# Spectral mixing kernel on one Trainium2 core: reordering at the three seams between its stages

## The reference

```
xf = rfft2(x, axes=(1, 2), norm='ortho')            # (4, 128, 65, 768), complex
o1 = relu(xf @ w1 + b1)                             # complex product, relu on each part
o2 = softshrink(o1 @ w2 + b2, 0.01)                 # complex product, per part
out = irfft2(o2, s=(128, 128), axes=(1, 2), norm='ortho') + x
```

## Time and profile before

| | us |
|---|---|
| median of 3 runs | 5172.28 (5172.27 to 5175.37) |
| profiled execution | 5172.48 |
| its span | 5170.2 |
| TensorE busy | 5031.5 |
| VectorE busy | 3993.2 |
| ScalarE busy | 2508.0 |
| GpSimd busy | 627.2 |

### The profile page before, as it was taken

How to read it: one execution, slowest core, us unless ns; L and a number is a source line. 1 busy time by engine, 2 the same in 40 slices (tenths; PEclk the granted TensorE clock), 3 DMA queues, 4 the chain that set the end, 5 groups by cost and what they waited for, 6 DMA issues and landing times.

```text
span 5170.2 us, 111909 instructions
## 1 busy us (share of the span) xinstructions
PE 5031.5 (97%) x43072; PEld 4143.5 (80%) x43072; DVE 3993.2 (77%) x5987; ACT 2508.0 (49%) x3649; POOL 627.2 (12%) x420
## 2 busy tenths in 40 slices
PE   7999999999999999999999999999999999999999
PEld 6887878888787887878878887888878778887887
DVE  6778777787777877778777787777787777877777
ACT  4554544545455454554445544445445455454543
POOL 0111011110111101111011110011110111101111
PEclk9999999999999999999999999999999999999999
DMA  3331233312333113332133321333312333123311
GB/s 107 99 99 36 73 100 99 104 44 61 100 99 104 50 54 99 99 104 61 44 100 99 104 74 43 87 99 104 89 41 74 99 104 99 44 61 99 103 50 50
DMA packets 1067748, 421.11 MB, mean 81 GB/s; under 512 B 1064864, under 2 KB 1064992, under 8 KB 1067168
## 3 DMA queue, kind: packets, MB, share of 16 engines
q1 hardware_dynamic: 1062432, 411.63, 30.1%
q10 hardware_dynamic: 4736, 1.60, 0.1%
HBM read 210.26 MB, written 201.33 MB: 80 GB/s over the span
## 4 chain that ended last, share of the span: by engine, by line
issue 88%; POOL 12%; POOLq 0%; DVE 0%
POOL x L926 12%; POOLq L925 0%; POOLq L929 0%; DVE x L855 0%; POOLq L926 0%; POOLq L938 0%
## 5 line engine op out<-in xcount | busy, mean ns | idle before, releaser
L926 POOL TENSOR_TENSOR x<-shrink_or_v,x 128x480 f32<-128x480 f32 (+1 forms) x416 | 627.0, 1507 | 4534.8 <-DVE shrink_or_v L848 4494.8
L543 PE MATMUL ps<-wts,hbig 128*128 128x192 f32 x4160 | 734.9, 327 | 4.3
L820 DVE TENSOR_TENSOR shrink_or_v<-ps,wts 128x768 f32<-128x768 f32 (+1 forms) x544 | 501.0, 921 | 281.5 <-PE ps L552 254.7
L773 DVE COPY ydg<-ps 128x512 f32<-128x512 f32 (+5 forms) x768 | 504.5, 657 | 250.8 <-PE ps L447 151.8
L447 PE MATMUL ps<-tab,ring 128*128 128x128 f32 x6144 | 694.6, 276 | 0.0
L447 PEld LDWEIGHTS ps<-tab,ring 128*128 128x128 f32 x6144 | 688.5, 192 | 5.4 <-DVE ring L894 5.4
L543 PEld LDWEIGHTS ps<-wts,hbig 128*128 128x128 f32 x4160 | 671.4, 190 | 16.5 <-ACT hbig L688 13.7
L434 PE MATMUL ps<-tab,ring 128*64 128x128 f32 x6144 | 681.6, 274 | 2.4 <-ACT ring L628 2.4
L435 PE MATMUL ps<-tab,ring 128*63 128x128 f32 x6144 | 681.6, 274 | 0.0
L434 PEld LDWEIGHTS ps<-tab,ring 128*64 128x64 f32 x6144 | 672.2, 137 | 7.3 <-ACT ring L628 4.2
L435 PEld LDWEIGHTS ps<-tab,ring 128*63 128x63 f32 x6144 | 672.1, 136 | 0.0
(11 more groups left out here) (71 smaller groups left out, 7507.0 us busy)
## 6 DMA issues: line engine op xcount, KB each, us to landing
out<-x SPq DMA_DIRECT2D x352, 480.0 KB, 4.6
x<-in_x SPq DMA_DIRECT2D x192, 768.0 KB, 7.9
x<-in_x SPq DMA_DIRECT2D x32, 816.0 KB, 8.1
x<-in_x SPq DMA_DIRECT2D x32, 720.0 KB, 6.4
out<-x SPq DMA_DIRECT2D x32, 432.0 KB, 4.2
wts<-in_mix SPq DMA_DIRECT2D x16, 513.0 KB, 3.6
out<-x SPq DMA_DIRECT2D x32, 240.0 KB, 4.4
out<-x SPq DMA_DIRECT2D x32, 192.0 KB, 4.3
```

What stands on the lines that cost most here:

```text
L543: mm = pe.matmul(o, hbig[:, k * H:(k + 1) * H], mix_part("w2_big"), start=first, stop=False, skip_group_check=True)
L773: dve.tensor_copy(*line_moves(stage, g)).then_inc(line_dve, 1)
L820: dve.tensor_tensor(parts(v), d, b2, ALU.add).then_inc(bias_done, 1)
L926: pool.tensor_tensor(xs[p][:, a:b, :], ucopy[g % 4][:, 0:b - a, :], mirror(xs[p], a, b), ALU.add).then_inc(plus_ready, 1)
```

## The change

- In pass it = 1 the second half of unit 1 is transformed ahead of mix1_whole of unit 0, not behind it; and mix1_whole waits for zsmall_ready only ahead of L501.
- The merge stands ahead of mix2_whole of the last unit, in the place of two keep_warm products; behind mix2_rows stand five keep_warm products and no longer the merge and three.
- The first row group runs over channels 0 to 87 (line groups 0 to 21) once these are moved, and over the other 8 channels when all are. Its signals come with the second part.
- The banks of the row groups, of row 0 and of the forward line groups are rotated by two, so that the first row group takes banks 2 and 3, those of inverse line groups 18 and 19.

```
+FIRST_LINES = 22
-        ROW0_BANK = 2
+        ROW0_BANK = 4
         def line_bank(stage, g):
             return (g + ROW0_BANK + 1) % 8 if stage == 0 else g % 8
+        def row_bank(g):
+            return 2 * ((g + 1) % 4)
...
-                def lines_moved(q, stage):
+                def lines_moved(q, stage, g=NG - 1):
                     for who in ("act", "dve"):
-                        pe.wait_ge(line_sems[who], moved_count(q, stage, NG - 1, who))
+                        pe.wait_ge(line_sems[who], moved_count(q, stage, g, who))
...
                 def mix1_whole(q, u):
                     pe.wait_ge(zbig_ready, NP * q + last_part(u))
-                    pe.wait_ge(zsmall_ready, NU * q + u + 1)
                     pe.wait_ge(zhi_ready, NU * q + u + 1)
...
                     pe.wait_ge(zlo_ready, NU * q + u + 1)
+                    pe.wait_ge(zsmall_ready, NU * q + u + 1)
...
                 def rows(q, g):
-                    bank = 2 * (g % 4)
+                    bank = row_bank(g)
...
+                def first_rows(q):
+                    a, b = odd_rows(0)
+                    c = LINE_GROUPS[FIRST_LINES][0]
+                    v, u = (ps[:, row_bank(0) + i, 0:n * CB].rearrange("p (h c) -> p h c", c=CB)
+                            for i, n in ((1, b - a), (0, HG)))
+                    yv, yu = ydg[:, HC + a - 1:HC + b - 1, :], ydg[:, 0:HG, :]
+                    lines_moved(q, 1, FIRST_LINES - 1)
+                    pe.matmul(v[:, :, 0:c], mat("inv_w_odd"), yv[:, :, 0:c], start=True, stop=True)
+                    pe.matmul(u[:, :, 0:c], mat("inv_w_even"), yu[:, :, 0:c], start=True, stop=True)
+                    lines_moved(q, 1)
+                    pe.matmul(v[:, :, c:CB], mat("inv_w_odd"), yv[:, :, c:CB], start=True, stop=True).then_inc(v_done, 1)
+                    pe.matmul(u[:, :, c:CB], mat("inv_w_even"), yu[:, :, c:CB], start=True, stop=True).then_inc(u_done, 1)
...
                                 pe.wait_ge(w1lo_ready, t + 1)
+                            if it == 1:
+                                fwd_big(q, it, 1)
                             if it >= 1:
                                 mix1_whole(q, it - 1)
-                            if (it, 1) in PARTS:
+                            if it != 1 and (it, 1) in PARTS:
                                 fwd_big(q, it, 1)
...
                         mix1_rows(q, NU - 1)
-                        keep_warm(q, 2)
+                        merge(q)
                         mix2_whole(q, NU - 1)
                         mix2_rows(q, NU - 1)
-                        merge(q)
-                        keep_warm(q, 3)
+                        keep_warm(q, 5)
                         inverse_lines(q)
-                        lines_moved(q, 1)
-                        for g in range(NF):
+                        first_rows(q)
+                        for g in range(1, NF):
                             rows(q, g)
...
-                    u, v = (ps[:, 2 * (g % 4) + i, 0:HG * CB].rearrange("p (h c) -> p h c", c=CB) for i in (0, 1))
+                    u, v = (ps[:, row_bank(g) + i, 0:HG * CB].rearrange("p (h c) -> p h c", c=CB) for i in (0, 1))
```

## The result

| | us |
|---|---|
| before, median of 4 runs | 5173.64 (5172.27 to 5175.37) |
| after, median of 4 runs | 5122.28 (5120.02 to 5126.10) |
| ratio, after to before | 0.9902, 95% interval 0.9889 to 0.9916 |
| profiled execution of after | 5123.14, its span 5120.9 |

The change makes the kernel faster by 1.0%. Profiled execution against profiled execution it is 49.3 us, where the sum forecast 72.4. The time is 22 us above the forecast of 5100 and 0.3 us outside the range.

The account below looks back on a forecast made before the run. TensorE, busy 97% of the span at full clock, was taken as the bound; 53.4 + 3 + 1.6 + 14.4 = 72.4 us off the profiled 5172.48 gave 5100, range 5085 to 5122.

Parts of the forecast that it names:

- What bounds the kernel, and the sign: TensorE, busy 97% at full clock, gains only from its waits or unneeded work; faster by over 0.2% at 0.95.
- Rivals 1, 3 and 4: Stall moved to L501, 5122, 8%; merge ahead of last mix2 stalls, 5183, 2%; moves bound otherwise, 5170, 3%.
- rival 2: Split of the first row group gives nothing, short passes eating the wait's gain: 14 us less, 5114; chance 12%.
- rival 1: TensorE stands at L501 because the two remainders come later than now: 22 us back, about 5122; chance 8%.
- First seam: H transform and first mixing: reordering and the later wait gain 1.67 us a step, bounds 1.50 and 1.80, 53.4 in all.
- Even steps: VectorE's earlier folds shorten TensorE's L468 waits for the small remainder: 3 us of 5.3 in all, bounds 0 and 5.3.
- Second seam: Edges, merge ahead of the last mix2_whole: between -0.1 and +0.15 us a step, taken 0.05, 1.6 in all.
- Third seam: First row group split to hide the last move's wait: 0.45 us a step, bounds 0.08 and 0.72, 14.4 in all.
- The cover of keep_warm: Ahead of the inverse lines, five keep_warm end before the tail pack, costing nothing; without that cover, 1.12 us.

Follow-up runs that it names:

- h_only: The kernel before with only unit 1's second half moved ahead of the first mixing and the small remainder's wait placed later: 5132.84 us, ratio 0.9920.
- rot: The kernel after with VectorE's loop turned, so the jump back lies behind the even step's three folds of unit 1: 5103.69 us, ratio 0.9867.
- spread: The kernel after with the third fold moved from unit 1 to unit 2 and later folds one unit on: 5102.71 us, ratio 0.9863.
- m_only: The kernel before with only the merge moved ahead of the last mix2_whole and five keep_warm behind: 5175.71 us, ratio 1.0003.
- nomerge: spread with the merge back in its old place, behind mix2: 5101.15 us, ratio 0.9861.
- r_only: The kernel before with only the split of the first row group and the rotated banks: 5160.65 us, ratio 0.9974.
- nosplit: spread with the first row group undivided, the banks still rotated: 5115.66 us, ratio 0.9888.
- nowarm: spread without the five keep_warm products ahead of the inverse lines: 5124.03 us, ratio 0.9907.
- light: The kernel after with each of the eight transfers of a later load cut to one row of H: 5102.88 us, ratio 0.9866.

## Why the prediction was right and where it failed
- **What bounds the kernel, and the sign:** right. TensorE's waits were the thing to look at, and both large ones went, with no new one at L501 (now L507), L494 (L499) or in front of the last mixing. Rivals 1, 3 and 4 did not come about, nor did rival 2: the rows gain. That rival 1 had put the time at 5122, where it came out, is a coincidence: its stall at L501 isn't there, and the time was lost in another place.
- **First seam:** forecast 1.67 a step, bounds 1.50 and 1.80. Measured 1.75 on the timeline and 1.82 over a step's mixing in h_only, at the upper bound. The timeline shows where the difference lies: the 16 passes of unit 1 now stand together and take 1.81 us (1487.30 to 1489.11) where the sum had 0.99 + 0.98, and the mixing behind them takes 2.27 where it had 2.19. That fits a change of weight width which now falls behind the mixing and no longer into the second half.
- **Even steps: this is the step that failed.** It read "VectorE's start on the folds comes earlier by more than TensorE's need does, so I take 3 us of the 5.3". VectorE was indeed free 1.19 us earlier against TensorE. But I took the 1.85 us of waiting for nothing in the earlier trace rows as a constant. It is the loop's jump, whose length depends on the loads, less what still runs beside it: 3.73 in the same step after, and the folds began 0.7 us later, not 1.2 earlier. I had weighed late loads only as data for the folds, by their issue and landing, and that was right: rot's first fold finds its rows in place. As traffic beside an instruction fetch they did not occur to me. The term was forecast at +3 us and measured at about -20: the even mixing's excess over the odd one went from 0.14 to 1.40 us, 16 x 1.26 = 20.2, and moving one fold gave 19.6 us back (spread's 5102.71 against after's 5122.28). Those 23 us are all of the miss. The other terms were off by +4.8, -4.2 and -1.3 us (first, second, third seam, over 32 steps), and that these nearly cancel is luck. My bounds for the even steps' term were 0 and 5.3; nothing excluded a loss, and I had put 0 as the lower end.
- **Second seam:** forecast +0.05 a step, bounds -0.10 and +0.15. Measured -0.05 (m_only) and -0.08 to -0.09 (nomerge), near the lower bound. The step that was off is "some 0.11 of it is to be had": the pack also waits for the last shrink, as the same sentence said, and only 0.05 was to be had. The price, 0.13 us of a later shrink, was the upper end given.
- **Third seam:** forecast 0.45, measured 0.42 (r_only) and 0.41 (nosplit). The wait of 0.62 went to the full. The price of the short passes was read too low: 0.36 us up to the next product and 0.08 more on it, 0.44 in all and so 0.11 for each of the four, not the 0.09 that I took from L418. With 0.44 the sum of the prediction gives 0.40. The Trainium skill's rule (TensorE: Matmul & The Clock Gate, LDWEIGHTS) gave 0.43 and a gain of 0.41, and the trace agrees with it: three of the four passes are 0.11 apart, and the first's missing 0.08 is what the next product has over its like.
- **The cover of keep_warm** ("cost nothing; without that cover they would cost 1.12 us"): nowarm's even steps show them free, and its odd ones what they buy.

By terms of a step, then: 1.82 + 0.41 - 0.08 = 2.15 where the even steps' stall is absent, and 2.13 was measured in odd steps; less 1.4 x 16 in even ones.

**Left open.** How the loads delay the fetch at the jump. It may stand behind transfers of the loads on the DMA engines; that the packet comes as the loads end speaks for it. Or it may stand behind an earlier packet of its own queue that the loads have delayed: in the slow jumps that packet lies 4.4 to 5.2 us ahead of the jump, in the two quick ones 5.4 and 5.6, in light 6.6 to 6.7. No run tells these apart. Why the clock fell in 11 steps of nowarm and not in the other 21 with the same pause is open too.

## What to carry to other kernels
Idle time that the profile gives to "issue" on an engine with a loop is not a constant: look whether it recurs once per loop body, check by the sequencer's records whether it is the price of the jump back, and ask what transfers will be under way when the engine gets there after the change. A gain on the bounding engine moves every other engine in time, so an order that had slack of a few tenths (here three folds ahead of a remainder) must be costed again; moving one fold brought 20 us back, and next to nothing before. Where an idle stretch is filled with dummy products, take them away only with the granted clock of the stretch behind in view.

## What the runs showed of the hardware
- The jump back at VectorE's loop costs 2.8 to 3.0 us from the branch to the next instruction with the DMA engines quiet (light, rot), and 4.2 to 5.1 us where the loads run on at 303 to 326 GB/s in the second microsecond behind it (12 of after's 14 jumps). The packet that follows it is 8 KB. Part of the cost hides behind an instruction that was issued before the jump: 1.25 us before, 0.60 after.
- A pause of 1.44 us of TensorE ahead of the inverse lines was followed by a granted clock of 0.51 for 3.4 us in 11 of 32 steps of nowarm, 1.63 us lost each time, and by 1.00 in the others. Across the whole span that is a mean clock of 0.996, hardly seen in the page's slices.
- Two passes of 32 and two of 40 columns on 128 weight columns are 0.03, 0.11, 0.11 and 0.11 us from start to start (after, L598 and L599), and the first product behind them takes 0.08 us more than its like.
